# Graph layer on one core: k/v pairs ahead of the edge loop, node mixing inside it, and feed-forward rows added into the output by scatters

## The reference, cut to what matters

```python
# x: 12500 x 256, 200000 edges; gat: 4 heads of 64; mix: 8 heads of 32; ffn: 256 -> 1024 -> 256
xn = _layernorm(x)
# gat: xp = xn @ W; per edge alpha = leaky_relu(a_src[src] + a_dst[dst]), softmax over the edges of dst
# (self loops included), agg = sum of w * xp[src]; out = elu(agg + bias)
# mix: qkv = xn @ w_qkv + b_qkv; k, v layer-normalised per head
kv = jnp.einsum('bhnd,bhne->bhde', k, v) / HW          # one 32 x 32 matrix per head, over all nodes
ret = jnp.einsum('bhnd,bhde->bhne', q, kv) + xn
mix = gelu(ret @ w1 + b1) @ w2 + b2 + xn
x2 = x + gat + mix
z = _layernorm(x2)
# ffn: weights = z @ wr + br; the 6249 nodes of largest weight are selected
y = (gelu(z[sel] @ f_w1 + f_b1) @ f_w2 + f_b2) * weights[sel]
out = x2 + z + processed                               # processed: y in selected rows, 0 elsewhere
```

## Time and profile before

| | |
|---|---|
| median of 3 executions | 3796.64 us (3795.04 to 3800.68) |
| the profiled execution's own time | 3800.68 us |
| its span | 3798.9 us |
| busy in the span: PE, DVE, ACT, POOL | 2163.0, 1977.0, 1222.0, 2361.8 us |
| share of the span | 57%, 52%, 32%, 62% |
| mean granted clock of PE | 0.774 of full |
| POOL's edge gathers L1140 | 1632, 1548.1 us busy |

### The profile page before, as it was taken

How to read it: one execution, slowest core, us unless ns; L and a number is a source line. 1 busy time by engine, 2 the same in 40 slices (tenths; PEclk the granted TensorE clock), 3 DMA queues, 4 the chain that set the end, 5 groups by cost and what they waited for, 6 DMA issues and landing times. The chain is left out here.

```text
span 3798.9 us, 44702 instructions
## 1 busy us (share of the span) xinstructions
PE 2163.0 (57%) x8039; PEld 1564.6 (41%) x8039; DVE 1977.0 (52%) x4888; ACT 1222.0 (32%) x3798; POOL 2361.8 (62%) x2430
## 2 busy tenths in 40 slices
PE   4652036766656656666666566552555554108998
PEld 3441014544434434444444344431333332007887
DVE  6672046656556555455565555543888888301111
ACT  2321033334333333333333333321555554002221
POOL 5776567777777777777777777751444443273443
PEclk7866558888887878878888788775767776559999
DMA  5642244444444444444444444432555554001111
GB/s 179 189 133 84 33 105 121 116 118 120 117 121 117 120 121 117 123 118 118 121 121 121 122 118 124 117 85 58 155 157 158 157 158 134 24 1 50 58 53 47
DMA packets 273849, 418.52 MB, mean 110 GB/s; under 512 B 85679, under 2 KB 190416, under 8 KB 273552
## 3 DMA queue, kind: packets, MB, share of 16 engines
q0 software_dynamic: 103008, 263.89, 27.1%
q1 hardware_dynamic: 170672, 153.14, 12.9%
HBM read 328.13 MB, written 88.71 MB: 110 GB/s over the span
## 5 line engine op out<-in xcount | busy, mean ns | idle before, releaser
L1140 POOL DMA_INDIRECT G<-tab_d,sidx x1632 | 1548.1, 949 | 538.4 <-issue 481.4
L1887 PE MATMUL bank<-G,ident 128*128 128x264 f32 x3264 | 926.4, 440 | 508.4 <-DVE G L1544 420.5
L1887 PEld LDWEIGHTS bank<-G,ident 128*128 128x128 f32 x3264 | 664.1, 215 | 811.1 <-issue 466.4
L1560 DVE TENSOR_TENSOR acc<-acc,bank 128x264 f32 x816 | 348.2, 427 | 260.9 <-PE bank L1887 231.2
L1863 PE MATMUL bank<-kvw,shared 128*128 128x512 f32 x392 | 244.6, 756 | 292.9 <-DVE shared L1481 271.7
L1760 ACT ACTIVATE G<-G,work 128x64 f32<-128x64 f32 x1632 | 394.4, 333 | 0.1
L1544 DVE TENSOR_TENSOR G<-G,bank 128x1024 f32<-128x1024 f32 x306 | 367.3, 1214 | 1.8
L656 PE MATMUL bank<-G 128*128 128x256 f32 x392 | 174.4, 622 | 209.5 <-DMA G<-xnT_d 209.5
L1481 DVE TENSOR_TENSOR shared<-bank,bkv 128x512 f32<-128x512 f32 x98 | 67.7, 691 | 387.0 <-issue 367.1
L1734 ACT ACTIVATE bank<-shared 128x512 f32<-128x512 f32 x98 | 58.9, 601 | 585.0 <-DVE shared L1481 585.0
L1863 PEld LDWEIGHTS bank<-kvw,shared 128*128 128x128 f32 x392 | 80.2, 227 | 396.6 <-DVE shared L1481 313.2
(11 more groups left out here) (378 smaller groups left out, 3546.2 us busy)
## 6 DMA issues: line engine op xcount, KB each, us to landing
G<-tab_d,sidx POOLq DMA_INDIRECT x1632
accP_d<-acc SPq DMA_DIRECT2D x100, 132.0 KB, 2.6
tab_d<-acc SPq DMA_DIRECT2D x49, 260.0 KB, 3.2
acc<-x_in SPq DMA_DIRECT2D x49, 256.0 KB, 3.6
xnT_d<-acc SPq DMA_DIRECT2D x49, 256.0 KB, 2.2
shared<-xnT_d SPq DMA_DIRECT2D x49, 256.0 KB, 2.8
G<-x_in SPq DMA_DIRECT2D x49, 256.0 KB, 4.8
G<-tab_d SPq DMA_DIRECT2D x49, 256.0 KB, 4.9
```

What stands on the lines that cost most here:

```text
L1140: g.indirect_dma_start(out=G[:, s, t, 0:TR], out_offset=None, in_=tab_d, in_offset=bass.IndirectOffsetOnAxis(ap=sidx[:, s, t:t + 1], axis= ...
L1560: v.tensor_tensor(a, a, bank[1 + i % NSB][:, 0:ROW], ALU.add).then_inc(sum_added, 1)
L1887: last = te.matmul(bank[1 + i % NSB][:, 0:ROW], ident[:, :], G[:, s, i * IT + k, :], start=(k == 0), stop=(k == IT - 1))
```

## The change

Constants follow from the sizes: KVC = 22, NK0 = 27, NKA = 15, MIX0 = 24.

- Stage A: xt and xrow have four slots instead of two.
- Barrier 1 is gone; each engine waits for the stores and scatters that it needs. Barriers 2 and 3 become one, and there are two in all.
- 27 k/v pairs come before the edge loop, in two buffers (the second lies in the first columns of acc), two banks of products and two of squares: pairs 0 to 14 right after stage A, pairs 15 to 26 after ACT's list copies and node terms. acc is cleared in two parts around them. The other 22 pairs are in chunks 0 to 21, both biases at the chunk's start.
- Chunk 22 loads the small arrays and chunks 22 and 23 fold the mix weights.
- Chunks 24 to 47 make two pairs each (chunk 48 one) of up, Gelu, down with b2 - 1 by a product of one row, x * std + mean terms, and their sum, stored as mix_d.
- The node stage has no PE work; it loads mix_d and tab_d rows (those of the first two pairs before the barrier), and stores z and out. x2 takes two operations, DVE's normalised rows go to ACT, the row weights are computed one step later, and POOL's L591 goes.
- The FFN gathers z only; DVE multiplies, and the scatter adds into out, which already holds x2 + z.

The core of the diff:

```diff
+    KVC = 2 * FIXED - (NP - 1) // 2 - 2
+    NK0 = NP - KVC
+    NKA = 15
+    MIX0 = KVC + 2
+    FREE = KVC * IC // (W // IT)
     RW = W + 2 * HG + 2
...
+        kv_at = (kv, accf[:, 0:4 * D].rearrange("p (a n) -> p a n", a=2))
+        xtk_at = (xtk, accf[:, 4 * D:6 * D].rearrange("p (k n) -> p k n", k=2))
+        KVCOLS = -(-6 * D // ROW) * ROW
+        pbank, qbank = (bank[7], bank[3]), (bank[0], bank[4])
...
-            with eng.Fori(0, FIXED) as r:
-                body(2 * r, 0, r, True)
-                body(2 * r + 1, 1, r, True)
-            body(2 * FIXED, 0, FIXED, False)
+            with eng.Fori(0, KVC // 2) as r:
+                body(2 * r, 0, r, "kv")
+                body(2 * r + 1, 1, r, "kv")
+            body(KVC, 0, KVC // 2, "fold0")
+            body(KVC + 1, 1, KVC // 2, "fold1")
+            with eng.Fori(KVC // 2 + 1, FIXED) as r:
+                body(2 * r, 0, r, "mix")
+                body(2 * r + 1, 1, r, "mix")
+            body(2 * FIXED, 0, FIXED, "mix_last")
...
-                for view, rows in ((z_v, zz), (base_v, bb), (out_v, bb)):
+                for view, rows in ((z_v, zz), (out_v, bb)):
...
                 dve.wait_ge(e_out, q + 1)
-                dve.wait_ge(o_mm, q + 1)
                 dve.wait_ge(b_ready, q + 1)
-
-                ck(v.scalar_tensor_tensor(x2[:, s], t2[:, s], 1.0, bank[3 + s][:, :].rearrange("p (t n) -> p t n", t=2), ALU.min, ALU.add))
+                ck(v.scalar_tensor_tensor(x2[:, s], t2[:, s], 1.0, xm_in[:, s], ALU.min, ALU.add))
+                v.sem_inc(x_read, 1)
                 ck(v.scalar_tensor_tensor(x2[:, s], t1[:, s], 0.0, x2[:, s], ALU.max, ALU.add))
-                dve.wait_ge(x_ready, q + 1)
-                ck(v.tensor_tensor(x2[:, s], x2[:, s], t3[:, s], ALU.add))
-                v.sem_inc(x_read, 1)
-
                 for t in (0, 1):
...
-                ck(v.reciprocal(mv2[:, :, 1], var2[:, 2:4]))
-                dve.wait_ge(b_out[s], 48 * r + 48)
-                for t in (0, 1):
-                    last = v.tensor_scalar(zz[:, s, t, :], x2[:, s, t, :], mv2[:, t, 0:1], mv2[:, t, 1:2], ALU.subtract, ALU.mult)
-                ck(last)
-                v.sem_inc(z_ready, 1)
-                for t in (0, 1):
-                    ck(v.scalar_tensor_tensor(junk, zz[:, s, t, :], 1.0, wrr, ALU.mult, ALU.mult, accum_out=wnode[:, ds(2 * q + t, 1)]))
+                ck(v.reciprocal(mv2[:, s, :, 1], var2[:, 2:4]))
+                v.scalar_tensor_tensor(mv2[:, s, :, 0], mv2[:, s, :, 0], -1.0, mv2[:, s, :, 1], ALU.mult, ALU.mult).then_inc(zs_ready, 1)
+                if not isinstance(q, int) or q:
+                    node_weight(q - 1, 1 - s)
+                if not more:
+                    node_weight(q, s)
                 assert ck.n == KNB, ck.n
 
...
-            def add_b2(q, s):
-                pool.wait_ge(x_scaled, q + 1)
-                g.tensor_tensor(t3[:, s], t3[:, s], b2r[:, None, :].to_broadcast([P, 2, D]), ALU.add).then_inc(x_ready, 1)
...
+                act.wait_ge(zs_ready, q + 1)
+                act.wait_ge(b_out[s], 32 * r + 32)
+                for t in (0, 1):
+                    last = a.activation(zz[:, s, t, :], x2[:, s, t, :], ACT.Identity, bias=mv2[:, s, t, 0:1], scale=mv2[:, s, t, 1:2])
+                last.then_inc(z_ready, 1)
...
-                    g.indirect_dma_start(out=out, out_offset=rows_at(q, t), in_=yo[:, q % 2, t, :], in_offset=None).then_inc(f_out[q % 2], 16)
-                if q + 2 < NQ:
-                    gather(bl, base_d, q + 2, b_in)
+                    g.indirect_dma_start(out=out, out_offset=rows_at(q, t), in_=yo[:, q % 2, t, :], in_offset=None,
+                                         compute_op=ALU.add).then_inc(f_out[q % 2], 16)
...
-                    ck(v.scalar_tensor_tensor(yo[:, s, t, :], ty[:, t, :], perm[:, ds(2 * q + t, 1), 1], bl[:, s, t, :], ALU.mult, ALU.add))
+                    ck(v.tensor_scalar(yo[:, s, t, :], ty[:, t, :], perm[:, ds(2 * q + t, 1), 1], None, ALU.mult))
...
+            for q in range(NKA + 2):
+                if q >= 2:
+                    sp.wait_ge(kv_mm, 2 * q - 2)
+                load_xt(q, q % 2)
+            sp.wait_ge(row_out, 16 * NB)
+            sp.sem_inc(pace, 1)
...
+                if mode == "fold0":
+                    sp.wait_ge(kv_acc, NP + 1)
+                    landed()
+                    load_mix(sp)
+                    load_turned(0, 0)
+                    load_turned(1, 1)
...
+                for m, k in pairs_in(c, mode):
+                    settled(sp, mix_ready, m + 3)
+                    sp.dma_start(mix_v[ds(m, 1)].rearrange("a p t n -> p (a t) n"), xm[:, k]).then_inc(mix_out[k], 16)
+                for m, k in pairs_in(c, mode)[0:following]:
+                    settled(sp, mix_out[k], 16 * (c - MIX0) + 16)
+                    load_raw(m + 2, k)
...
-            barrier(pool, 1)
+            for s in range(4):
+                pool.wait_ge(tab_out[s], 16 * ((NP - s + 3) // 4))
+            pool.wait_ge(dummy_out, 16)
+            pool.sem_inc(pace, 1)
...
+            def first_kv(lo, hi):
+
+                for q in range(lo, hi):
+                    for t in (0, 1):
+                        add_bias(q, t, max(q, 1), q % 2)
+                    if q > lo:
+                        norm_kv(q - 1, kk, (q - 1) % 2)
+                    for t in (0, 1):
+                        reduce_squares(q, t, kk)
+                norm_kv(hi - 1, kk, (hi - 1) % 2)
+
+            first_kv(0, NKA)
+            for s in range(4):
+                dve.wait_ge(tab_out[s], 16 * ((NP - s + 3) // 4))
+                dve.wait_ge(xt_out[s], 16 * ((NP - s + 3) // 4))
+            v.memset(accf[:, KVCOLS:], 0.0)
+            dve.wait_ge(row_out, 16 * NB)
+            v.memset(G[:, 0, :, TR:ROW], 0.0)
+            dve.wait_ge(flat_done, 2)
+            stage(0, 0)
+            dve.wait_ge(flat_done, 3)
+            stage(1, 1)
+            first_kv(NKA, NK0)
+            dve.wait_ge(kv_acc, NK0 + 1)
+            lk(v.memset(accf[:, 0:KVCOLS], 0.0))
+            dve.wait_ge(flat_done, NB // 14)
+            v.memset(G[:, 1, :, TR:ROW], 0.0)
+            assert kk.n == KKV * NK0
 
...
+            def add_mixed(m, k):
+                dve.wait_ge(t3_ready, m + 1)
+                dve.wait_ge(m_down, m + 3)
+                v.tensor_tensor(xm[:, k], xm[:, k], dbank[k][:, :].rearrange("p (t n) -> p t n", t=2), ALU.add).then_inc(mix_ready, 1)
...
                 if with_kv:
-                    add_bias(q, 0)
+                    add_bias(q, 0, q + 1, 0)
+                    add_bias(q, 1, q + 1, 0)
+                for m, k in pairs_in(c, mode):
+                    v.tensor_copy(sc1[:, k], stat[:, ds(2 * m, 2), :]).then_inc(sc_ready, 1)
                 dve.wait_ge(rows_in[s], 16 * CT * u + 16 * CT)
                 dve.wait_ge(flat_done, NB // 14)
...
+            first_kv(0, NKA)
+            act.wait_ge(row_out, 16 * NB)
+            act.sem_inc(pace, 1)
...
+            def mix_up(m, k, c):
+                pe.wait_ge(xtm_in[k], 16 * (c - MIX0) + 16)
+                pe.wait_ge(m_act, m + 1)
+                for f in (0, 1):
+                    for i in (0, 1):
+                        last = te.matmul(ubank[k][:, f * D:f * D + D], wm[:, i, f * P:f * P + P], xtm[k][:, i, :], start=(i == 0), stop=(i == 1))
+                last.then_inc(m_up, 1)
+
+            def mix_down(m, k):
+                pe.wait_ge(m_act, m + 3)
+                pe.wait_ge(mix_ready, m + 1)
+                for t in (0, 1):
+                    part = dbank[k][:, t * D:t * D + D]
+                    te.matmul(part, ones[0:1, :], b2row[0:1, :], start=True, stop=False)
+                    for i in (0, 1):
+                        last = te.matmul(part, hT[:, k, i, t * P:t * P + P], w2m[:, i, :], start=False, stop=(i == 1))
+                last.then_inc(m_down, 1)
...
+            for q in range(NK0):
+                for t in (0, 1):
+                    kv_product(q, t, q % 2, q // 2 + 1)
+                if q:
+                    kv_sums(q - 1, (q - 1) % 2)
+            kv_sums(NK0 - 1, (NK0 - 1) % 2)
```

526 lines of the change are left out of this document (261 added, 265 removed).

## The result

The change takes **3747.22 us**, the median of 4 runs (3745.32 to 3749.67), beside 3797.36 for the kernel before in as many (3795.04 to 3800.68): a ratio of 0.9868, interval 0.9851 to 0.9885. That is 50 us less, where 19 were forecast: clear of noise, and more than twice the forecast. The profiled execution took 3749.06 us, with a span of 3747.2. Lines of the kernel after are used from here on: L1475 is the bias of a k/v pair, L1481 its reductions, L1493 its scaling, L1924 its products, L1932 to L1936 its sums, L1149 a row gather, L535 to L538 `weights_of`, L553 the node weights, L562 and L564 the two x2 operations, L602 POOL's scaled sums, L611 its bb, L637 ACT's Identities.

The account below looks back on a forecast made before the run. POOL's gathers were taken to bound the edge loop, so its end follows gather list 2. Terms 182 - 41 - 5 - 154 - 1 = -19 gave 3778 us against the median 3796.64, range 3695 to 3840.

Parts of the forecast that it names:

- part 3: Node stage: a step takes 8.5 us instead of 11.71, over 48 steps -154 us.
- part 1: 27 k/v pairs ahead of the edge loop: cycle 13.0 us, gather list 2 at 752 against 570, +182 us.
- part 2: Mix weights move into chunks 22 and 23: -41 us; node stage starts with its rows loaded: -5 us.
- part 5: Edge-loop chunks: DVE's 36.3 us (k/v) and 39.1 us (mix) both stay under POOL's 40.1, 0 us.
- part 4: FFN: two fewer gathers at its start save 2.5 us, a later last accumulating scatter costs 1.5: -1 us.
- What bounds the kernel: POOL's gathers bound the edge loop, 1.253 us each; no engine is full in the node stage; PE in the FFN.
- Rival (a): Pairs ahead of the loop: PE keeps the full clock, cycle 9.9 us, 74 us less, 3704; chance 0.18.
- Rival (b): Pairs ahead of the loop: PE stays at the low clock, cycle 15.8 us, 67 us more, 3845; chance 0.12.
- Rival (d): Node step: POOL blocks DVE under every two-operand operation, step 9.7 us, 58 us more, 3836; chance 0.11.

Follow-up runs that it names:

- combo_c: The change with PE's next product before the sums, NKA = 17, bb on ACT and POOL's scaled sums held back: 3607.42 us, ratio 0.95, faster kind.
- warm_c: The change with 7 idle matmuls on PE in each of the 27 pairs ahead of the loop: 3728.04 us, ratio 0.9813, faster kind.
- nka9_c: The change with NKA = 9 instead of 15, so 9 pairs before the list copies and 18 behind: 3768.02 us, ratio 0.9918, faster kind.
- pe_order: The change with PE issuing the next pair's first product before the sums of the pair before: 4943.95 us, slower kind.
- z_dve: The change with the node stage's normalised rows back on DVE: 5100.77 us, slower kind, where the kernel before took 4876.14.
- node_only: The kernel before with four slots and the node stage's edits, bb on ACT, scaled sums held back, mixing not moved: 3673.35 us, ratio 0.9675, faster kind.
- four_slots: The kernel before with only xt and xrow in four slots: 4869.46 us to 4876.14, ratio 0.9989, slower kind.
- bb_late: The change with bb on ACT and POOL's scaled sums held back until DVE is through x2: 3705.93 us, ratio 0.9758, faster kind.

## Why the prediction was right and wrong

The sign and the way the time goes were right, and the time lies in the range. The size of the gain was wrong: it was forecast at 19 us and is 50. Of the missing 33 (in spans) 21.5 are in part 3, 20.5 in part 1, 2.5 in part 2, while part 5 takes back 8.7 and part 4 3.2. So the steps that failed are two terms of the sum: the node step, put at 8.5 us with a hold by POOL in it that the new order doesn't have, and measured at 8.05; and the start of list 2, put at +182 with a cycle of 13.0 and 12 us of stage A, and measured at +161.5 with 12.5 and 18.3. Each was off by an eighth or so, both in the same direction, and the forecast was their small difference.

**What bounds the kernel: right.** The loop's end follows the start of list 2. List 2 lay at 570, 626, 707, 732 and 749 in before, `combo_c`, `warm_c`, the change and `nka9_c`, and the last gather at 2534, 2599, 2683, 2704 and 2721: 1964 behind it in before, 1972 to 1975 in the others. (That holds for the faster kind; in the slower one POOL waits 889.6 us for PE and is not the bound.) DVE's extra work in the mix chunks is free, as said in part 5: POOL's waits for PE come to 17.9 us over the loop, for 15.2 before.

**Part 1: the mechanism right, the cycle put too large and stage A's gain too small.** The cycle is serial between PE and DVE, at a mixed clock: 0.73 for the expected 0.72. That figure is in part luck: it was borrowed from a stage where PE works 53% of the time, while here it works 76%, and with 89% and 86% (`warm_c`, `combo_c`) the clock is 0.80 and 0.92, so the share of busy time doesn't give it. It was put at 12.3 and raised to 13.0 for squares of ACT that come late; it is 12.5. Of the 0.7 there is 0.2. 24 x 0.5 makes 12 us. Stage A gave 18.3 instead of 12: I took a value below POOL's row of waits, 16.0 us, and it gave a little more than the row. That is 6. Some 2 us are in the ends of the two groups.

Rival (a), full clock, is refuted as stated; but `pe_order` and `combo_c` show that a fast cycle can be had by filling PE's pause with its own next product: 8.2 us at 0.92. Rival (b) fell too: that PE was at the lower level before the loop said nothing of a PE that works 76% of the time.

**Part 2: right**, -41 for -41, and -7.5 for -5 at the node stage's start.

**Part 3, the larger miss: the sum had a stretch in it that isn't there.** The step was put at 9.03 with both weights at 2.38 *and* the small operation at 1.05, so POOL beside DVE was counted twice, and a value between 7.7 and 9.03 taken. In the trace only one operation in a step is held, L535 by L611, for about as much in the mean (1.04) as L519 was before (1.05), while L553 has its own 0.43. The 2.38 of the earlier trace rows held 1.0 (1.41 for 0.43) that belonged to POOL's old place. 9.03 - 0.98 is 8.05, and the step is 8.05. I had written "without, 7.06" in the same paragraph; the experiments reach it (7.19) once POOL's one remaining operation runs under statistics. Against 8.5 the 48 steps give 22 us more.

Rival (d) had the rule right and the reach wrong. The Trainium skill ("GPSIMD Engine Reference", Key points) says that the two engines contend where a DVE instruction runs in a 2-port perf mode or has two SBUF inputs, and `z_dve` shows the second for x2: 1.71 and 2.27 instead of 0.69. Whether L559, with one operand, was held for the first isn't shown. But in the change x2 and POOL's tensor operations overlap only in the first steps, so L562 and L564 keep their 0.69 and the contention costs one small operation a step. A timeline of both engines says which; the rule alone doesn't. The prediction misread one row here: L539's plain 0.69 says nothing of its operand in PSUM, for it begins at 2922.05, when POOL's L587 has ended (2921.99), and in none of the steps of the kernel before does it run beside a POOL tensor operation.

**Part 4: right within 3 us.** From the last x2 to the end it is 588.6 us, where it was 586.4. The accumulating stores are issued in 1593 ns, for 986 of the plain ones in `node_only`, and POOL is idle in front of them for 209 us, so that they have room; a run without them wasn't made.

**Part 5: 0 for +8.** DVE isn't it. Each of the 1568 gathers takes 5 ns more on POOL itself (954 to 949; 947 in `node_only`), and does from the first chunk on, before any mixing (735 to 1620: 670.78 / 704 = 953 ns): 7.8 us. The kernels with pairs ahead and mixing in the loop have it in both kinds of batch (952 to 956), the kernel before, `four_slots` and `node_only` have not (945 to 949). What in them lengthens an issue by 5 ns wasn't isolated.

**And the question that the forecast did not ask.** The change is two changes, and one of them loses (all of this in the faster kind). The node stage's edits and the four slots give 124 us by themselves (`node_only`, which has the better place for POOL's work as well). Hiding the mixing under the gathers, with that same place (`bb_late`), takes 33 us back: it pays 191 in the pairs moved ahead and the longer gathers, and earns 157 by weights and steps. Whether the node stage's edits give as much with POOL's work where the change has it wasn't tried. It paid with PE's order mended and two more pairs under the scatter, in `combo_c`: the last gather is then 87.5 us after that of `node_only` instead of 191, and the kernel 66 us faster.

## What to carry to other kernels

Work that is hidden under a bound engine still has to make room there. Price what it pushes out in front, in serial cycles, before counting what it saves behind, and run the two halves of such a change apart. Between VectorE and GpSimd it is the moment that counts: put GpSimd's tensor operation beside the statistics of VectorE, the one work seen here that it doesn't hold, and look at the timeline of both for whatever is stretched next. When a serial pair of engines leaves TensorE a pause, give it its own next product first: that shortened a cycle from 12.5 to 8.2 us here, of which filling the pause with idle matmuls got only 0.9.

## What was not expected of the hardware

- **Batches differ, and with them the sign.** The same kernel took 3797 us in some and 4879 in others, where cycles and steps agree and the difference is in stalls of the gather loop (59 us a chunk for 40) and of straight stretches (73.31 us, no releaser recorded). The change is 1.3% faster in the one kind and 2.9% slower in the other. Chip number 10 is in both kinds; the cause is open.
- **POOL holds DVE where they meet.** 8 columns cost 1.22, 1.06 or 0.17 us, and 512 cost 0.69, 1.71 or 2.27, by what POOL runs at that moment. One-operand normalised rows of 256 columns took 0.81 for 0.40. Statistics under the same POOL operation keep their 0.75.
- **The granted clock in the pairs** was 0.73, 0.80 and 0.92 with PE busy 76, 89 and 86% of the time (the change, `warm_c`, `combo_c`): the busier of the last two has the lower clock.
- **An accumulating scatter** of the FFN's rows is issued in 1.59 us, a plain one in 0.99.
- **A gather's issue** got 5 ns longer (949 to 954) in the kernels with pairs ahead of the loop, worth 8 us in all; what does it is open.
